# A new order for the opening of a decoder layer on one core: keys, values, queries, with identity products first

## The chip, the cores and the metric

The kernel runs on one core of a Trainium2 chip. The metric is device microseconds of one execution; the median of several runs is compared. TensorE (PE), VectorE (DVE), ScalarE (ACT), GpSimd (POOL) and the DMA queues of SyncE (SP) and ScalarE work in parallel and wait for each other through semaphores.

## The reference

Input x is 16 sequences of 128 tokens of 128 numbers. Four stages follow each other, each with a residual and a layer norm: a gated convolution mixer, a decoder block of self-attention and cross-attention (16 heads of 64) with a feed-forward of 512, and a last feed-forward with one expert for each of the first 16 tokens. The change concerns the mixer, at the start of the kernel:

```python
x = jnp.einsum('bld,de->ble', u, W_in) + b_in
x = jnp.swapaxes(x, 1, 2)
uc = dw_causal_conv(x, short_w, short_b)
q, k, v = (uc[:, :D], uc[:, D:2 * D], uc[:, 2 * D:])
v = k * v
v = dw_causal_conv(v, inner_w, inner_b)
y = q * v
y = jnp.swapaxes(y, 1, 2)
return jnp.einsum('bld,de->ble', y, W_out) + b_out
```

## The kernel before, in words

One block holds five instruction streams, written out by hand, one for each engine; each runs strictly in its written order, so the order of the lines is the schedule. Sequences go through the mixer in 8 pairs m (two sequences, 256 columns) and through the attentions as items n = 0 to 31 (16 of self-attention, then 16 of cross-attention).

Input projection and three-tap convolution of the mixer are one operation: VectorE multiplies W_in by each tap (`first_weights`, L1162), and nine matmuls per part c (three taps; each product in three, of high and low halves of fp32) add up in one PSUM bank (`projection`, L608 to L610). Part 0 are the queries, 1 the keys, 2 the values. Operands are split into a rounded high half, by ScalarE (`w_hi` L969, `x_high` L872, `weight_high` L903), and a low rest, by VectorE (`first_weights_low` L1168, `x_low` L1155, `weight_low` L1239).

A pair then goes like this: ScalarE copies each part out of its bank into C with the bias (`projected`, L881); GpSimd corrects the first two columns of all three parts (L1565) and multiplies keys by values into KV (`keys_values`, L1569); VectorE runs the four-tap inner convolution into G (`inner_convolution`, L1194, L1198); GpSimd multiplies the queries into yT (`gate`, L1576); TensorE makes the output product (`mixer_output`, L622), into the bank of the keys; VectorE adds the residual (`mixer_residual`, R, L1207), to which GpSimd has added the output bias (`output_bias`, L1583), and takes the moments (L1214 to L1221); GpSimd raises to the power -1/2 (`mixer_deviation`, L1591); VectorE makes the shift (`mixer_shift`, L1227), ScalarE the normalised rows N (L891); TensorE transposes them (L634), ScalarE and VectorE take the high and low halves x1 (L899, `x1_low` L1234). The units of the first items follow (`unit`, L72 to L74: two head pairs of queries or keys for two items), copied out by ScalarE (queries, L827) and VectorE (keys, `k_out`, L1099); with the key units of the first two turns comes `scores(0)` (L551), then `maxima` on VectorE (L1081), which adds the mask `maskb` (made at L1402), and so on through a loop over the items, in which pairs 3 to 7 of the mixer are woven in.

The three parts of a pair use two banks: queries bank 4, keys bank 5, values bank 4 again. So the values of a pair wait for the copy of its queries, and a pair waits for the copies of the one before:

```python
C_BANK, OUT1_BANK, X1T_BANK = (4, 5, 4), 5, W_BANK
wait(pe, c_ok, (3 * m, 3 * m, 3 * m + 1)[c])
```

The opening of TensorE is: projections of pair 0, then of pair 1, output product of pair 0, projections of pair 2, transposes of pair 0, output product of pair 1, eight units, scores of item 0. Small bias terms (`tap_biases`, `first_biases`, L1173 to L1184) are VectorE's, between the weights.

## Time and profile before

| | us |
|---|---|
| median of 3 runs (501.26 to 502.74) | 501.43 |
| the profiled execution, its time | 501.12 |
| its span in the trace | 499.2 |
| TensorE busy in the span | 470.6 (94%) |
| VectorE busy | 385.0 (77%) |
| ScalarE busy | 366.8 (73%) |
| GpSimd busy | 251.9 (50%) |

The time of the execution has about 1.9 us around the span of the trace. All later times count from the start of the span. TensorE's digits in the slices of the page stand at 4, 7 and 8 for the first three slices (37 us) and at 9 from the fourth to the last but two; DMA is at 8, 7 and 4 tenths in the first three slices and near nothing after them, with two exceptions.

### The profile page before, as it was taken

The page shows a single profiled execution, that of the slowest core. Times are in us where ns is not written, and L with a number is a line of the kernel's source. Part 1 is how long each engine was busy: PE and PEld are TensorE (multiplying, and loading weights), DVE is VectorE, ACT ScalarE, POOL GpSimd, SP SyncE. Part 2 cuts the span into 40 slices and gives each one's busy share as a digit, 9 for nine tenths or more (in the row PEclk, how much of TensorE's full clock was granted, in tenths as well). Part 3 has the DMA queues.
Part 4 walks back from the last instruction along what each step waited for, and adds up shares of the span by engine and source line. Part 5 has one row for each costly group of instructions (what it writes and reads, how often), then busy time and mean ns, then how long its engine had stood idle before and what let it go on. Part 6 is the DMA issues. An engine that isn't in the chain of part 4 may idle for free.

```text
span 499.2 us, 14097 instructions
## 1 busy us (share of the span) xinstructions
PE 470.6 (94%) x4644; PEld 431.5 (86%) x4644; DVE 385.0 (77%) x1852; ACT 366.8 (73%) x1390; POOL 251.9 (50%) x342
## 2 busy tenths in 40 slices
PE   4788999999999999999999999999999999999894
PEld 4678889999999999999999999999999997798672
DVE  4768778898888877887787777777777777538866
ACT  3547887868677788877778887777777777836763
POOL 1545357675565654555545454444554455633432
PEclk9999999999999999999999999999999999999987
DMA  8740000000000004000000000000000000400003
GB/s 242 233 195 2 1 3 1 2 2 2 1 3 1 2 2 126 1 4 1 3 1 2 2 2 1 3 1 3 3 1 3 1 2 3 169 1 0 7 13 90
DMA packets 15720, 14.18 MB, mean 28 GB/s; under 512 B 2848, under 2 KB 13344, under 8 KB 15520
## 3 DMA queue, kind: packets, MB, share of 16 engines
q1 hardware_dynamic: 14080, 12.81, 8.2%
q8 instruction: 38, 0.62, 0.5%
q10 hardware_dynamic: 1568, 0.47, 0.5%
q14 instruction: 34, 0.28, 0.2%
HBM read 12.10 MB, written 1.18 MB: 27 GB/s over the span
## 4 chain that ended last, share of the span: by engine, by line
PE 73%; DVE 13%; ACT 5%; issue 3%; DMA 2%; POOL 2%; SPq 1%; POOLq 0%; DVEq 0%; ACTq 0%
PE late_bank L582 10%; PE late_bank L534 10%; PE late_bank L551 10%; PE late_bank L566 10%; PE late_bank L72 8%; PE late_bank L74 8%; PE late_bank L73 8%; ACT P L817 3%; DVE P L1081 3%; DMA x<-in_xT 2%; PE late_bank L591 1%; DVE G L1198 1%; DVE ffstats L1253 1%; PE late_bank L608 1%; PE late_bank L610 1%
## 5 line engine op out<-in xcount | busy, mean ns | idle before, releaser
L817 ACT ACTIVATE P<-P,at_negmax 128x128 f32<-128x128 f32 x512 | 198.9, 396 | 79.1 <-DVE at_negmax L1081 79.1
L1530 POOL TENSOR_TENSOR P<-P,at_inv 128x512 f32<-128x512 f32 x128 | 136.6, 1078 | 123.2 <-DVE at_inv L1091 123.1
L1107 DVE COPY at_PT<-late_bank 128x512 f32<-128x512 f32 x128 | 87.7, 688 | 35.1 <-PE late_bank L534 34.9
L1081 DVE CUSTOM_DVE_ANT_0 P<-late_bank,maskb 128x128 f32<-128x128 f32 x512 | 110.5, 286 | 2.7 <-PE late_bank L551 2.7
L817 ACT ACTIVATION_READ_ACCUMULATOR P<-P,at_negmax 128x1 f32 x512 | 100.1, 195 | 0.0
L534 PE MATMUL late_bank<-ident,P 128*128 128x128 f32 x512 | 76.4, 273 | 2.0 <-DVE at_negmax L1081 1.0
L534 PEld LDWEIGHTS late_bank<-ident,P 128*128 128x128 f32 x512 | 59.8, 140 | 8.5 <-issue 4.0
L551 PE MATMUL late_bank<-at_k,at_q 64*128 64x128 f32 x1024 | 65.8, 278 | 0.9 <-DVE at_k L1099 0.9
L551 PEld LDWEIGHTS late_bank<-at_k,at_q 64*128 64x128 f32 x1024 | 59.7, 188 | 4.8 <-issue 1.2
L566 PE MATMUL late_bank<-at_PT,V 128*64 128x128 f32 x1024 | 63.0, 276 | 0.0
L566 PEld LDWEIGHTS late_bank<-at_PT,V 128*64 128x64 f32 x1024 | 55.2, 137 | 3.9
L1099 DVE COPY at_k<-late_bank 128x512 f32<-128x512 f32 x64 | 44.2, 691 | 8.1 <-PE late_bank L74 7.0
L1081 DVE DVE_READ_ACCUMULATOR2_ANT at_negmax<- 128x1 f32 x512 | 42.7, 83 | 0.0
L827 ACT ACTIVATE at_q<-late_bank 128x512 f32<-128x512 f32 x64 | 37.7, 589 | 4.0 <-PE late_bank L74 4.0
L1548 POOL TENSOR_TENSOR at_N<-at_N,row_ln_g 128x128 f32<-128x128 f32 x32 | 14.7, 460 | 49.8 <-DVE at_N L1132 49.8
L836 ACT ACTIVATE V<-late_bank 128x512 f32<-128x512 f32 x64 | 37.6, 587 | 0.0
L844 ACT ACTIVATE at_OT<-late_bank 128x512 f32<-128x512 f32 x64 | 34.3, 587 | 2.9 <-PE late_bank L566 2.9
L608 PE MATMUL late_bank<-xT_hi,w_hi 128*128 128x256 f32 x72 | 22.8, 317 | 11.2 <-DVE xT_lo L1155 7.1
L582 PE MATMUL late_bank<-wo_sa,at_OT 128*128 128x128 f32 x256 | 31.3, 276 | 0.6 <-DVE x1T_lo L1234 0.6
L582 PE MATMUL late_bank<-wo_ca,at_OT 128*128 128x128 f32 x256 | 31.2, 275 | 0.0
L582 PEld LDWEIGHTS late_bank<-wo_sa,at_OT 128*128 128x128 f32 x256 | 29.9, 192 | 1.0 <-issue 1.0
L582 PEld LDWEIGHTS late_bank<-wo_ca,at_OT 128*128 128x128 f32 x256 | 29.9, 192 | 0.1
(195 smaller groups left out, 1055.4 us busy)
## 6 DMA issues: line engine op xcount, KB each, us to landing
ctxT_raw<-in_ctxT SPq DMA_DIRECT2D x1, 1024.0 KB, 8.8
out<-xres SPq DMA_DIRECT2D x4, 224.0 KB, 2.6
x<-in_xT SPq DMA_DIRECT2D x1, 768.0 KB, 9.5
xres<-in_x SPq DMA_DIRECT2D x1, 768.0 KB, 14.0
tap_rows<-in_short_wT SPq DMA_DIRECT2D x3, 192.0 KB, 4.9
sa_wq_raw<-in_sa_wq SPq DMA_DIRECT2D x1, 512.0 KB, 7.4
sa_wk_raw<-in_sa_wk SPq DMA_DIRECT2D x1, 512.0 KB, 8.5
sa_wv_raw<-in_sa_wv SPq DMA_DIRECT2D x1, 512.0 KB, 9.8
```

The source lines that it names most:

```text
L72: nc.tensor.matmul(out, w.hi[wsel], x.hi[xsel], start=first, stop=False)
L73: nc.tensor.matmul(out, w.hi[wsel], x.lo[xsel], start=False, stop=False)
L74: return nc.tensor.matmul(out, w.lo[wsel], x.hi[xsel], start=False, stop=True)
L534: last = nc.tensor.transpose(banks[T_BANK[g % 2]][:, h * 128:(h + 1) * 128], P[:, n % 2, HQ * g + h, :], k.ident[:])
L551: last = nc.tensor.matmul(score_bank(h), q[rows, t % 2, h // 2, pair], kk[rows, t % 2, h // 2, pair], start=True, stop=True)
L566: last = nc.tensor.matmul(banks[O_BANK[h // 8]][part:part + 64, h // 2 % 4 * 128:(h // 2 % 4 + 1) * 128], V[:, n % 2, h * DH:(h + 1) * DH] ...
L582: last = nc.tensor.matmul(banks[W_BANK][:, 0:128], OT[:, n % 2, c, :], out_w[att(n)][:, c, :], start=(c == 0), stop=(c == H // 2 - 1))
L817: last = nc.scalar.activation(P[:, n % 2, h, :], P[:, n % 2, h, :], ACT.Exp, scale=-1.0, bias=negmax[:, n % 2, h:h + 1], accum_out=total[: ...
L1081: last = nc.vector.tensor_tensor_reduce(P[:, n % 2, h, :], score_bank(h), k.maskb[:, cols(n)], scale=1.0, scalar=3.0e38, op0=ALU.add, op1= ...
L1099: nc.vector.tensor_copy(kk[:, t % 2, u - 1:u + 1, :], banks[UNIT_BANK[1]][:].rearrange("p (h l) -> p h l", h=2)).then_inc(k_ok, 1)
L1107: nc.vector.tensor_copy(PT[:, HQ * g:HQ * g + HQ, :], banks[T_BANK[g % 2]][:].rearrange("p (h l) -> p h l", h=HQ)).then_inc(pt_ok, 1)
L1530: nc.gpsimd.tensor_tensor(tile, tile, inv[:, n % 2, HQ * g:HQ * g + HQ].unsqueeze(2).to_broadcast([128, HQ, 128]), ALU.mult).then_inc(norm ...
```

## The change

The parts of the first three pairs go in the order keys, values, queries (`FIRST_ORDER`), in all engines, with weights, taps and loads in that order too. For these pairs each part has a bank of its own (keys 5, values 4, queries bank 6, the bank of the attention's values), and a part waits for the copy of the same part of the pair before. Twelve products of the identity with itself stand ahead of the first projection, into bank 3. The edge correction is done in two instructions, keys and values ahead of their product, queries ahead of the gate, in all eight pairs. The small bias operations go to GpSimd. The output product of pair 0 stands between values and queries of pair 1, that of pair 1 after the first query unit. The other engines' lists are reordered accordingly; the mask operation moves from before the first convolution to between two key copies.

```diff
-        C_BANK, OUT1_BANK, X1T_BANK = (4, 5, 4), 5, W_BANK
+        C_BANK, FIRST_C_BANK, OUT1_BANK, X1T_BANK = (4, 5, 4), (V_BANK, 5, 4), 5, W_BANK
+        FIRST_PAIRS, FIRST_ORDER = 3, (1, 2, 0)
+        def place(m, c):
+
+            return 3 * m + (FIRST_ORDER.index(c) if m < FIRST_PAIRS else c)
...
-            for n in SA[:2]:
-                sp.dma_start(k.raw[n][:], io[n]).then_inc(ld_w[n], 16)
             tokens = io["x"].rearrange("b p d -> p b d")
+            sp.dma_start(k.raw[SA[0]][:], io[SA[0]]).then_inc(ld_w[SA[0]], 16)
             sp.dma_start(k.xres[:, 0:GRP], tokens[:, 0:GRP]).then_inc(ld_xres[0], 16)
+            sp.dma_start(k.raw[SA[1]][:], io[SA[1]]).then_inc(ld_w[SA[1]], 16)
...
-                wait(pe, c_ok, (3 * m, 3 * m, 3 * m + 1)[c])
+                if m < FIRST_PAIRS:
+                    wait(pe, c_ok, place(m - 1, c) + 1)
+                else:
+                    wait(pe, c_ok, (3 * m, 3 * m, 3 * m + 1)[c])
...
             pe.wait_ge(ident_ok, 1)
+            for _ in range(12):
+                nc.tensor.matmul(banks[3][:, 0:128], k.ident[:], k.ident[:], start=True, stop=True)
             pe.wait_ge(pads_ok, 2)
-            for m in (0, 1):
-                for c in range(3):
-                    projection(-1, m, c)
+            for c in FIRST_ORDER:
+                projection(-1, 0, c)
+            projection(-1, 1, 1)
+            projection(-1, 1, 2)
             mixer_output(-1, 0)
-            for c in range(3):
-                projection(-1, 2, c)
+            projection(-1, 1, 0)
+            projection(-1, 2, 1)
             x1_transposes(-1, 0)
+            projection(-1, 2, 2)
+            unit(-2, 0)
             mixer_output(-1, 1)
-            for j in range(4):
+            projection(-1, 2, 0)
+            for j in range(1, 4):
                 unit(-2, j)
...
+            nc.scalar.dma_start(w_out[:], io["W_out"]).then_inc(ld_tok, 16)
+            row_broadcast(nc, act, b_out[:], io["b_out"]).then_inc(ld_tok, 16)
             row_broadcast(nc, act, k.mask_raw[:], io["mask"].rearrange("b p -> (b p)")).then_inc(ld_mask, 16)
-            row_broadcast(nc, act, b_out[:], io["b_out"]).then_inc(ld_tok, 16)
-            nc.scalar.dma_start(w_out[:], io["W_out"]).then_inc(ld_tok, 16)
...
             x_high(1)
-            for c in range(3):
+            for c in FIRST_ORDER:
                 projected(0, c)
+            weight_high(SA[0])
+            projected(1, 1)
+            projected(1, 2)
             x_high(2)
-            weight_high(SA[0])
-            for c in range(3):
-                projected(1, c)
+            projected(1, 0)
             weight_high(SA[1])
-            projected(2, 0)
+            mixer_normal(0)
             projected(2, 1)
-            mixer_normal(0)
+            x1_high(0)
             projected(2, 2)
-            x1_high(0)
-            x_high(3)
             weight_high(SA[2])
             q_out(-2, 0)
+            projected(2, 0)
+            x_high(3)
...
+            def edges(m, parts):
+                count = parts.stop - parts.start
+                part = C[:, m % 2, parts, :, 0:2]
+                nc.gpsimd.tensor_tensor(part, part, edge[:, parts].unsqueeze(2).to_broadcast([128, count, PAIR, 2]),
+                                        ALU.add).then_inc(fix_ok, 1)
...
-                pool.wait_ge(c_ok, 3 * (m + 1))
-                part = C[:, m % 2, :, :, 0:2]
-                nc.gpsimd.tensor_tensor(part, part, edge[:].unsqueeze(2).to_broadcast([128, 3, PAIR, 2]),
-                                        ALU.add).then_inc(fix_ok, 1)
-                pool.wait_ge(fix_ok, m + 1)
+                pool.wait_ge(c_ok, 3 * m + (2 if m < FIRST_PAIRS else 3))
+                edges(m, np.s_[1:3])
+                pool.wait_ge(fix_ok, 2 * m + 1)
...
+                pool.wait_ge(c_ok, 3 * (m + 1))
+                edges(m, np.s_[0:1])
+                pool.wait_ge(fix_ok, 2 * (m + 1))
                 pool.wait_ge(g_ok, m + 1)
...
-            pool.wait_ge(edge_ok, 2)
+            pool.wait_ge(zeros_ok, 1)
+            tap_biases()
             keys_values(0)
+            gate(0)
             output_bias(0)
-            gate(0)
```

VectorE, from the second x split of the opening to the residual of pair 0 and on to the low half of x1 (the rows of the moments are left out; `xT_lo` is a split of x, `sa_wq_lo` of the query weights, `sa_wk_lo` of the key weights; what stands in brackets is what the instruction waits for). Before:

```order
L1155 TENSOR_TENSOR xT_lo<-x1,xT_hi 128x2x128 [waits mx_xhi]
L1402 TENSOR_SCALAR maskb<-mask_raw 128x2048 [waits mx_ld_mask]
L1194 TENSOR_SCALAR G<-KV,inner,inner_b 128x256 [waits mx_ld_inner,mx_kv_ok]
L1198 SCALAR_TENSOR_TENSOR G<-KV,inner,G 128x256 [waits mx_g_part] x3
L1155 TENSOR_TENSOR xT_lo<-x1,xT_hi 128x2x128 [waits mx_xhi]
L1239 TENSOR_TENSOR sa_wq_lo<-sa_wq_raw,sa_wq_hi 128x1024 [waits mx_w_hi]
L1207 TENSOR_TENSOR R1<-late_bank5,xres 128x256 [waits mx_xb_ok,mx_o1_mm]
L1194 TENSOR_SCALAR G<-KV,inner,inner_b 128x256 [waits mx_y_ok,mx_kv_ok]
L1198 SCALAR_TENSOR_TENSOR G<-KV,inner,G 128x256 [waits mx_g_part] x3
L1227 SCALAR_TENSOR_TENSOR shift1<-mv1,rstd1 128x2 [waits mx_rstd1_ok]
L1239 TENSOR_TENSOR sa_wk_lo<-sa_wk_raw,sa_wk_hi 128x1024 [waits mx_w_hi]
L1234 TENSOR_TENSOR x1T_lo<-late_bank7,x1T_hi 128x256 [waits mx_x1hi]
```

and now:

```order
L1191 TENSOR_TENSOR w3_lo<-w3_raw,w3_hi 128x3x128 [waits mx_whi]
L1201 TENSOR_SCALAR G<-KV,inner,inner_b 128x256 [waits mx_ld_inner,mx_kv_ok]
L1205 SCALAR_TENSOR_TENSOR G<-KV,inner,G 128x256 [waits mx_g_part] x3
L1246 TENSOR_TENSOR sa_wq_lo<-sa_wq_raw,sa_wq_hi 128x1024 [waits mx_w_hi]
L1214 TENSOR_TENSOR R1<-late_bank5,xres 128x256 [waits mx_xb_ok,mx_o1_mm]
L1178 TENSOR_TENSOR xT_lo<-x1,xT_hi 128x2x128 [waits mx_xhi]
L1234 SCALAR_TENSOR_TENSOR shift1<-mv1,rstd1 128x2 [waits mx_rstd1_ok]
L1201 TENSOR_SCALAR G<-KV,inner,inner_b 128x256 [waits mx_y_ok,mx_kv_ok]
L1205 SCALAR_TENSOR_TENSOR G<-KV,inner,G 128x256 [waits mx_g_part] x3
L1241 TENSOR_TENSOR x1T_lo<-late_bank7,x1T_hi 128x256 [waits mx_x1hi]
L1246 TENSOR_TENSOR sa_wk_lo<-sa_wk_raw,sa_wk_hi 128x1024 [waits mx_w_hi]
```

The mask operation is gone from here, the shift stands ahead of the second convolution instead of behind it, and the low half of x1 behind that convolution, ahead of the key weights.

VectorE again, from the residual of pair 1 to the first scores (the moments left out again; `at_k` are the key copies, `sa_wv_lo` the value weights). Before:

```order
L1207 TENSOR_TENSOR R1<-late_bank5,xres 128x256 [waits mx_n1_ok,mx_xb_ok,mx_o1_mm]
L1099 COPY at_k<-late_bank1 128x512 [waits at_u_mm] x2
L1239 TENSOR_TENSOR sa_wv_lo<-sa_wv_raw,sa_wv_hi 128x1024 [waits mx_w_hi]
L1099 COPY at_k<-late_bank1 128x512 [waits at_u_mm]
L1227 SCALAR_TENSOR_TENSOR shift1<-mv1,rstd1 128x2 [waits mx_rstd1_ok]
L1099 COPY at_k<-late_bank1 128x512 [waits at_u_mm]
```

and now:

```order
L1214 TENSOR_TENSOR R1<-late_bank5,xres 128x256 [waits mx_n1_ok,mx_xb_ok,mx_o1_mm]
L1122 COPY at_k<-late_bank1 128x512 [waits at_u_mm]
L1246 TENSOR_TENSOR sa_wv_lo<-sa_wv_raw,sa_wv_hi 128x1024 [waits mx_w_hi]
L1122 COPY at_k<-late_bank1 128x512 [waits at_u_mm]
L1421 TENSOR_SCALAR maskb<-mask_raw 128x2048 [waits mx_ld_mask]
L1234 SCALAR_TENSOR_TENSOR shift1<-mv1,rstd1 128x2 [waits mx_rstd1_ok]
L1122 COPY at_k<-late_bank1 128x512 [waits at_u_mm]
L1178 TENSOR_TENSOR xT_lo<-x1,xT_hi 128x2x128 [waits mx_xhi]
L1122 COPY at_k<-late_bank1 128x512 [waits at_u_mm]
```

The value weights are one key copy earlier, and the mask operation and a split of x stand between the key copies.

TensorE around the output product of pair 0 (`late_bank5<-w_out,yT`). Before:

```order
L608 MATMUL late_bank4<-xT_hi,w3_hi 128x256
L609 MATMUL late_bank4<-xT_lo,w3_hi 128x256
L610 MATMUL late_bank4<-xT_hi,w3_lo 128x256
L622 MATMUL late_bank5<-w_out,yT 128x128 [waits mx_c_ok,mx_y_ok,mx_ld_tok]
L622 MATMUL late_bank5<-w_out,yT 128x128
L608 MATMUL late_bank4<-xT_hi,w3_hi 128x256 [waits mx_c_ok,mx_xlo]
```

and now:

```order
L621 MATMUL late_bank4<-xT_hi,w3_hi 128x256
L622 MATMUL late_bank4<-xT_lo,w3_hi 128x256
L623 MATMUL late_bank4<-xT_hi,w3_lo 128x256
L638 MATMUL late_bank5<-w_out,yT 128x128 [waits mx_c_ok,mx_y_ok,mx_ld_tok]
L638 MATMUL late_bank5<-w_out,yT 128x128
L621 MATMUL late_bank6<-xT_hi,w3_hi 128x256 [waits mx_c_ok]
```

Before, the product comes after the nine matmuls of pair 1's values and ahead of pair 2's queries, in bank 4. Now it comes ahead of pair 1's queries, in bank 6.

## Rows read from the trace of the kernel before

**Rows 1.** Windows: stretch, us, busy of PE, PEld, DVE, ACT, POOL, clock, DMA

```profile
7.00:12.00 5.00, 4.93 (x24) 4.96 (x25) 4.18 (x11) 2.19 (x5) 0.00 (x0) 1.00 1.01 358
34.00:60.00 26.00, 23.54 (x210) 21.61 (x211) 19.76 (x96) 20.04 (x81) 10.79 (x14) 1.00 0.00 1
60.00:450.00 390.00, 386.73 (x4039) 359.82 (x4038) 307.26 (x1521) 301.85 (x1217) 210.84 (x285) 1.00 0.04 11
```

**Rows 2.** Timeline of PE: start us, duration us, line, operation [idle before]

```profile
7.07 0.55 PE L608 MATMUL late_bank<-xT_hi,w_hi 128*128 128x256 f32 x1 [7.07 <-DVE xT_lo L1155]
...
11.47 0.39 PE L610 MATMUL late_bank<-xT_hi,w_lo 128*128 128x256 f32 x1
11.69 0.29 PE L608 MATMUL late_bank<-xT_hi,w_hi 128*128 128x256 f32 x1
11.81 0.28 PE L609 MATMUL late_bank<-xT_lo,w_hi 128*128 128x256 f32 x1
...
18.49 0.61 PE L622 MATMUL late_bank<-w_out,yT 128*128 128x128 f32 x4
...
24.86 0.39 PE L72 MATMUL late_bank<-x1T_hi,sa_wq_hi 128*128 128x256 f32 x1
...
34.09 2.06 PE L551 MATMUL late_bank<-at_k,at_q 64*128 64x128 f32 x32 [0.88 <-DVE at_k L1099]
```

**Rows 3.** The timeline of ACT in the opening

```profile
12.61 0.47 ACT L881 ACTIVATE C<-late_bank,conv_bias 128x256 f32<-128x256 f32 x1 [0.85 <-PE late_bank L610]
15.53 0.42 ACT L872 ACTIVATE xT_hi<-x 128x256 fp32r<-128x256 f32 x1 [2.44 <-DMA x<-in_xT]
```

**Rows 4.** The timeline of POOL in the opening

```profile
13.26 0.21 POOL L1565 TENSOR_TENSOR C<-C,edge 128x12 f32<-128x12 f32 x1 [10.61 <-ACT C L881]
13.55 0.74 POOL L1569 TENSOR_TENSOR KV<-C 128x256 f32<-128x256 f32 x1
...
16.77 0.84 POOL L1576 TENSOR_TENSOR yT<-C,G 128x256 f32<-128x256 f32 x1 [1.79 <-DVE G L1198]
...
20.65 0.81 POOL L1591 TENSOR_TENSOR rstd<-mv,half_neg 128x2 f32<-128x2 f32 x1 [0.38 <-DVE mv L1221]
22.53 1.71 POOL L1576 TENSOR_TENSOR yT<-C,G 128x256 f32<-128x256 f32 x1 [1.07 <-DVE G L1198]
```

**Rows 5.** The timeline of DVE in the opening

```profile
10.70 1.22 DVE L1402 TENSOR_SCALAR maskb<-mask_raw 128x2048 bf16<-128x2048 uint8 x1
...
16.94 1.75 DVE L1239 TENSOR_TENSOR sa_wq_lo<-sa_wq_raw,sa_wq_hi 128x1024 fp32r<-128x1024 f32 x1
19.13 0.42 DVE L1207 TENSOR_TENSOR R<-late_bank,xres 128x256 f32<-128x256 f32 x1 [0.44 <-PE late_bank L622]
...
20.48 0.41 DVE L1194 TENSOR_SCALAR G<-KV,inner,inner_b 128x256 f32<-128x256 f32 x1
20.93 1.52 DVE L1198 SCALAR_TENSOR_TENSOR G<-KV,inner,G 128x256 f32<-128x256 f32 x3
...
22.37 0.15 DVE L1227 SCALAR_TENSOR_TENSOR shift<-mv,rstd 128x2 f32<-128x2 f32 x1
22.44 1.22 DVE L1239 TENSOR_TENSOR sa_wk_lo<-sa_wk_raw,sa_wk_hi 128x1024 fp32r<-128x1024 f32 x1
...
26.19 0.43 DVE L1207 TENSOR_TENSOR R<-late_bank,xres 128x256 f32<-128x256 f32 x1 [0.68 <-issue]
...
27.53 0.69 DVE L1099 COPY at_k<-late_bank 128x512 f32<-128x512 f32 x1
29.28 0.69 DVE L1099 COPY at_k<-late_bank 128x512 f32<-128x512 f32 x1 [1.07 <-PE late_bank L74]
29.89 1.70 DVE L1239 TENSOR_TENSOR sa_wv_lo<-sa_wv_raw,sa_wv_hi 128x1024 fp32r<-128x1024 f32 x1
```

**Rows 6.** The line L446, the load of x for pair 1

```profile
L446 SPq DMA_DIRECT2D x<-in_xT x1: 486/486/486, 3.2 to 3.2; - x1
DMA to landing us min/median/max: 6.3/6.3/6.3
```

94 lines of the change are left out of this document (49 added, 45 removed).

## The prediction

> **What bounds the kernel now.** I read the windows by stage first, for the stage in which TensorE is not full. From 60 to 450 us it is busy for 386.7 of 390 us, so nothing can be won there by order; between 34 and 60 us 2.5 us are missing, and the opening before that is thin [rows 1]. Then the timeline of each engine from the start to the first scores. TensorE begins at 7.07 us, gives the first output product at 18.49, the first query unit at 24.86 and the first scores at 34.09 [rows 2]. What follows the scores hangs on them through relative waits only, all loads that it needs being long on their way, so I count what the change does to the 34.09 and carry it to the end.
>
> Along that path the reader is to see three things. The queries, keys and values of pair 0 are all needed before GpSimd may multiply keys by values: the third copy starts at 12.61, the product KV ends at 14.29 [rows 3, 4]. ScalarE then waits for the large x load until 15.53 [rows 3], with the copies of pair 1 queued behind it, and TensorE holds the first output product behind pair 1, though its operand yT is done at 17.61 [rows 2, 4]. Last, VectorE: its shift for the first layer norm is issued at 22.37, behind a whole convolution of pair 1 (20.48 to 22.45) [rows 5]. From 27.53 VectorE and TensorE hand each other key units, with waits such as the 1.07 us at 29.28 [rows 5].
>
> **The change, step by step.** Times are of the profiled execution.
>
> *Identity products.* They wait for the identity alone, and no row shows when they start. TensorE does nothing before 7.07 in any case. Two output products of the same shape and type leave four matmul records, spaced about like those of 256 columns (0.61 us for four, of which 0.28 is the last one's own) [rows 2]. So twelve make 24 records, at the early spacing of 0.22 (11.47 to 11.69) 5.3 us at most. So they should be over about when the first projection is ready, at the same 7.07 as before. Matmuls of 256 columns start 0.22 us apart up to 11.69, and 0.12 from there [rows 2]: the engine worked at half its rate (the 1.2 GHz level) for 4.6 us from its first matmul, then at the full one. If the products do that stretch, every projection costs 9 x 0.12 = 1.1 us instead of 9 x 0.21 = 1.9. Bounds: worth the whole of it, or nothing. I take the whole, since they are as long and as dense as the stretch that did it before.
>
> *Keys and values first.* The weights of the second part are combined, split and subtracted as before, without the small bias operations among them, but with the third part's combination (0.56) ahead of the second subtraction. I put the values' weights at 8.9, their product at 8.9 + 1.1 + 0.2 of drain = 10.2 and their copy (0.47) at 10.7. GpSimd needs only these two: 0.3 for the edge and 0.7 for KV [rows 4] give 11.9 against 14.29. The convolution takes 1.97 (20.48 to 22.45) [rows 5], to 13.9. The five small bias operations on GpSimd cost about 0.3 each by the spacing of its smallest one (13.26 to 13.55) [rows 4], 1.5 in all, before anyone needs them: nothing.
>
> *The port.* VectorE goes on at 13.9 with the low part of the query weights, GpSimd with yT. Where VectorE began first, its 1.22 (22.44) made yT take 1.71 (22.53); where GpSimd began first, yT took 0.84 and the weights 1.75 (16.77, 16.94) [rows 4, 5]. In the new order they stand next to each other and VectorE need not wait for a signal: I take 1.6 for yT, to 15.5; the other bound, 0.84, is a rival.
>
> *Output product between projections.* It comes at 15.6 instead of 18.49, so R at 16.3 instead of 19.13, 2.8 earlier; the bias addition that it also needs, as large as KV's product (0.7), follows yT and ends at 16.2. GpSimd's power ended at 21.46 (20.65 and 0.81), 2.33 behind the start of R, and the shift could have followed there [rows 4, 5]; it is now ahead of the convolution and comes 2.4 behind R, at 18.7. From shift to first query unit took 2.49 (22.37 to 24.86). Now the convolution of pair 1 stands between shift and the low part of x1, 18.7 + 1.97 + 0.42: again 21.2. The first unit is **3.7 us earlier**.
>
> *What is given back.* The residual of pair 1 waits for GpSimd's addition of the output bias, which stands behind keys times values of pair 2; and that product's projection now comes after the transposes, at 19.9, so its copy ends at 21.7. The key weights' 1.22 us on VectorE (from 21.1) then hold GpSimd's port; edge, KV and bias addition end at 24.1, R of pair 1 starts at 24.2 instead of 26.19: 2.0 earlier. The first key copy starts at 25.6 instead of 27.53.
>
> From there before: 6.56 us to the scores. Now: key copy 0.6, low value weights 1.2 (as at 22.44), key copy 0.6, then the **mask multiplication, 1.22, which before ran at 10.70 while VectorE had to wait for KV anyway** [rows 5] and here stands on the path, then as before from the end of the value weights (31.59) to the scores, 2.5. The moved x split (0.42) fits into the wait for the last key unit. Sum 6.1; if the mask operation begins beside a GpSimd addition, 0.45 more, as the 1.70 at 29.89 and the 1.75 at 16.94 against 1.22 show for the weights. So the scores start between 31.7 and 32.2. I take 32.2, since both long operations that stood beside GpSimd's were held: **1.9 us earlier**.
>
> By the Trainium skill (page "SBUF — State Buffer", section "SBUF: two separate sides") VectorE and GpSimd share a port pair as an exclusive lock, which a VectorE operation takes if it has two SBUF inputs or runs in a two-port mode; the mask operation has one input. By that rule it would be held only if its mode is such a one, and no row here shows it beside GpSimd. If it is not, the saving is 2.4.
>
> *Nothing for the rest.* The edge correction is now two GpSimd instructions per pair, 8 more in all at about 0.3. GpSimd is busy for 210.8 of 390 us [rows 1], and the added one runs before the convolution's result is there. Of the loads, first x of GRP sequences and key weights change places and the mask goes last of three: each is needed later than it lands. Should GpSimd be late all eight times, 2.4 us would be gone.
>
> Sum: 501.12 - 1.9 = 499.2 for the profiled execution. The median of the three runs stands 0.3 above it, at 501.43, so I forecast **499.5**. A measurement of this kernel tells about 0.3% (1.5 us) from no change; faster means below 499.9.
>
> **Rivals.**
>
> A. *The identity products do not raise the rate* before the projections. For: no row shows such products. Against: the rate changed once in the opening and stayed through the gaps after it. Then values follow keys at 9.1 to 11.1, KV is 1.1 later, and 0.8 are left: 500.6. Chance 0.14.
>
> B. *GpSimd gets the port.* If query weights reach ScalarE late, yT begins first and ends 0.9 earlier; with the mask operation not held, another 0.45. Up to 3.2 saved, 2.8 likely: 498.6. Chance 0.14.
>
> C. *The saving is taken up later.* The 2.5 us of missing TensorE time from 34 to 60 us [rows 1] may hide waits that do not move, or the added edge instructions fall on the path. 0.2 to 0.9 left: 500.8. Chance 0.12.
>
> D. *Slower: the second x pair.* On both ScalarE and VectorE the split of x of pair 1 now stands ahead of the copies and the query weights of pair 0. That load was issued at 3.2 and took 6.3, to 9.5 [rows 6], with the DMA engines full (share 1.01 from 7 to 12 us) [rows 1]. It decides from about 9.8, one for one: a landing at 11.7 leaves nothing, at 13.3 the kernel is 1.6 slower, 503.0. For: the rearranged queue of ScalarE loads beside it. Against: the mask's 256 KB, which ran beside it before, now follow 128 KB of others. Chance 0.05, with 0.02 more for anything else that is late.
>
> **How the numbers follow.** The main case has 0.53, with its own range of 499.0 to 500.0 from the bounds of the port and 0.3 us of seams in so long a chain. 498.4 to 501.2 takes in A, B and C with the spread of the runs; D is outside. Faster: 0.48 of the main case and B, 0.62. Same: the rest of the main case, A and C, 0.31. Slower: 0.07.
>
> **What would show it.** In the profile after: matmul spacing of 0.12 from the first projection (A if 0.21); first output product near 15.6, yT of 1.6 (B if 0.8); first query unit near 21.2; R of pair 1 near 24.2; the mask operation at 28 with 1.2 or 1.7; scores near 32.2, and every later landmark shifted by the same amount (C if less at 60 us than at 34). I am wrong if the output product is earlier but the scores are not, or if the first projection starts after 7.1 because the identity products still run.

## The result, and the profile after

| | before | after |
|---|---|---|
| median of 7 runs each, us | 501.43 (500.66 to 502.74) | 499.21 (497.63 to 501.00) |
| the profiled execution, its time and span | 501.12 / 499.2 | 499.44 / 497.6 |
| first scores of item 0 | 34.09 | 32.57 |

The ratio of the runs, after to before, is 0.9949, with a 95% interval of 0.9928 to 0.997: faster by 2.2 us, or between 0.3% and 0.7%. The forecast was 499.5.

The timeline of PE in the profile after, against [rows 2] (start us, duration us, line, operation, idle before):

```profile
1.56 5.49 PE L735 MATMUL late_bank<-ident 128*128 128x128 f32 x24 [1.56 <-POOL ident L1658]
7.23 0.55 PE L621 MATMUL late_bank<-xT_hi,w_hi 128*128 128x256 f32 x1 [0.18 <-DVE xT_lo L1178]
7.58 0.38 PE L622 MATMUL late_bank<-xT_lo,w_hi 128*128 128x256 f32 x1
7.80 0.28 PE L623 MATMUL late_bank<-xT_hi,w_lo 128*128 128x256 f32 x1
7.92 0.28 PE L621 MATMUL late_bank<-xT_hi,w_hi 128*128 128x256 f32 x1
...
15.78 0.68 PE L638 MATMUL late_bank<-w_out,yT 128*128 128x128 f32 x4 [1.72 <-issue]
...
21.36 0.39 PE L72 MATMUL late_bank<-x1T_hi,sa_wq_hi 128*128 128x256 f32 x1
...
32.57 0.68 PE L561 MATMUL late_bank<-at_k,at_q 64*128 64x128 f32 x7 [0.88 <-DVE at_k L1122]
```

The identity products fill 1.56 to 7.05. The first projection starts at 7.23; its first two matmuls still take 0.35 and 0.22 us to the next, and from 7.80 on they follow at 0.12 us. The output product comes 2.71 earlier, the first unit 3.50, the scores 1.52: more than half of the lead is given back between unit and scores.

The timeline of POOL, against [rows 4]:

```profile
10.94 0.20 POOL L1581 TENSOR_TENSOR C<-C,edge 128x8 f32<-128x8 f32 x1 [3.80 <-ACT C L903]
11.23 0.73 POOL L1592 TENSOR_TENSOR KV<-C 128x256 f32<-128x256 f32 x1
...
14.11 1.57 POOL L1602 TENSOR_TENSOR yT<-C,G 128x256 f32<-128x256 f32 x1 [1.12 <-DVE G L1205]
...
22.10 0.83 POOL L1581 TENSOR_TENSOR C<-C,edge 128x8 f32<-128x8 f32 x1 [0.32 <-ACT C L903]
23.02 0.74 POOL L1592 TENSOR_TENSOR KV<-C 128x256 f32<-128x256 f32 x1
23.71 0.73 POOL L1609 TENSOR_TENSOR xres<-xres,b_out 128x256 f32<-128x256 f32 x1
...
28.25 1.80 POOL L1627 TENSOR_TENSOR x<-N,row_ln_b 128x256 f32<-128x256 f32 x1
```

and of DVE, against [rows 5]:

```profile
5.01 0.56 DVE L1185 TENSOR_TENSOR w_raw<-w_in,tap_rows 128x384 f32<-128x384 f32 x1 [5.01 <-DMA tap_rows<-in_short_wT]
...
13.88 1.22 DVE L1246 TENSOR_TENSOR sa_wq_lo<-sa_wq_raw,sa_wq_hi 128x1024 fp32r<-128x1024 f32 x1
16.50 0.42 DVE L1214 TENSOR_TENSOR R<-late_bank,xres 128x256 f32<-128x256 f32 x1 [1.40 <-PE late_bank L638]
...
21.23 1.65 DVE L1246 TENSOR_TENSOR sa_wk_lo<-sa_wk_raw,sa_wk_hi 128x1024 fp32r<-128x1024 f32 x1
24.54 0.42 DVE L1214 TENSOR_TENSOR R<-late_bank,xres 128x256 f32<-128x256 f32 x1 [1.67 <-issue]
...
25.88 0.68 DVE L1122 COPY at_k<-late_bank 128x512 f32<-128x512 f32 x1
26.48 1.21 DVE L1246 TENSOR_TENSOR sa_wv_lo<-sa_wv_raw,sa_wv_hi 128x1024 fp32r<-128x1024 f32 x1
...
28.23 1.22 DVE L1421 TENSOR_SCALAR maskb<-mask_raw 128x2048 bf16<-128x2048 uint8 x1
29.37 0.70 DVE L1234 SCALAR_TENSOR_TENSOR shift<-mv,rstd 128x2 f32<-128x2 f32 x1
29.99 0.68 DVE L1122 COPY at_k<-late_bank 128x512 f32<-128x512 f32 x1
...
31.73 0.69 DVE L1122 COPY at_k<-late_bank 128x512 f32<-128x512 f32 x1 [0.72 <-PE late_bank L74]
```

KV ends at 11.96 instead of 14.29. Wherever a long weight split of VectorE meets GpSimd, one of the two is long: the query weights (13.88) begin first and yT takes 1.57; the key weights (21.23) take 1.65 beside the end of the second pair's yT, and the edge correction at 22.10 has 0.83 for eight columns' work. The mask operation at 28.23 took its plain 1.22, but GpSimd's addition beside it took 1.80, and the shift behind it, of 128 x 2 numbers, 0.70. The first row is the start of the whole chain: the moment at which the first taps land.

The windows from 34 us on (us, then busy of PE, PEld, DVE, ACT, POOL, clock, DMA), against [rows 1]:

```profile
34.00:60.00 26.00, 23.59 (x216) 21.65 (x214) 21.00 (x103) 21.52 (x84) 10.39 (x13) 1.00 0.01 2
60.00:450.00 390.00, 386.72 (x4019) 359.24 (x4017) 308.12 (x1525) 301.74 (x1215) 211.72 (x289) 1.00 0.04 11
```

Nothing changed there. The scores of items 0, 1 and 5 start at 32.57, 46.94 and 101.40 where they started at 34.09, 48.43 and 102.90: the lead stays at 1.5 us.

### The profile page after: what moved, and what is told of

The parts are those of the page before. It is cut to its first block, busy times and chain, and to the rows that moved or that the text cites. A ratio compares the mean times of both kernels' runs of the same rounds, so it can differ in the third digit from the quotient of the medians.

```text
span 497.6 us, 14153 instructions
## 1 busy us (share of the span) xinstructions
PE 471.0 (95%) x4668; PEld 433.1 (87%) x4668; DVE 384.3 (77%) x1847; ACT 366.9 (74%) x1390; POOL 257.2 (52%) x355
## 4 chain that ended last, share of the span: by engine, by line
PE 70%; DVE 15%; ACT 5%; issue 4%; DMA 2%; POOL 2%; SPq 1%; POOLq 0%; DVEq 0%; ACTq 0%
PE late_bank L592 11%; PE late_bank L544 10%; PE late_bank L561 10%; PE late_bank L576 10%; PE late_bank L72 8%; PE late_bank L74 8%; PE late_bank L73 8%; ACT P L839 3%; DVE P L1104 3%; DVE ffstats L1260 2%; PE late_bank L601 1%; DMA x<-in_xT 1%; PE late_bank L621 1%; PE late_bank L622 1%; PE late_bank L623 1%
## 5 line engine op out<-in xcount | busy, mean ns | idle before, releaser
L1114 DVE RECIPROCAL at_inv<-at_total 128x4 f32<-128x4 f32 x128 | 21.0, 170 | 9.4 <-ACT P L839 9.4
```

## The experiments

Single times lie up to 1 to 3 us from their median (once 4 us), as much as most of the effects, so the traces carry the verdicts, one traced execution for each kernel. A single trace has a scatter too: the first taps landed at 4.88 us in the trace before, at 5.01 in that after, and between 5.11 and 5.72 in the experiments. This table counts from that landing, VectorE's first product; when the first experiments were planned, landmarks were counted from the start of the span, and all expectations but that of e11 are in those times.

| | taps land | output product | first unit | R of pair 1 | first key copy | scores | median us (runs) | ratio to before, interval |
|---|---|---|---|---|---|---|---|---|
| before | 4.88 | 13.61 | 19.98 | 21.31 | 22.65 | 29.21 | 501.43 (7) | 1 |
| after | 5.01 | 10.77 | 16.35 | 19.53 | 20.87 | 27.56 | 499.21 (7) | 0.9949 (0.9928 to 0.997) |
| e1_no_identity | 5.32 | 11.81 | 18.77 | 21.37 | 22.71 | 29.42 | 501.56 (10) | 1.0005 (0.9986 to 1.0025) |
| e2_kv_waits_all | 5.44 | 11.65 | 20.19 | 25.77 | 27.11 | 34.07 | 506.56 (4) | 1.0101 (1.0057 to 1.0145) |
| e3_product_behind | 5.11 | 10.51 | 16.94 | 19.50 | 20.84 | 27.54 | 499.58 (10) | 0.9969 (0.9941 to 0.9998) |
| e4_two_banks | 5.44 | 10.64 | 16.22 | 19.39 | 20.73 | 27.42 | 499.52 (10) | 0.9959 (0.9935 to 0.9983) |
| e12_biases_back | 5.63 | 10.64 | 16.22 | 19.40 | 20.74 | 27.43 | 500.82 (10) | 0.9982 (0.9959 to 1.0005) |
| e5_mask_late | 5.56 | 10.52 | 16.64 | 19.38 | 20.72 | 26.82 | 498.87 (9) | 0.9941 (0.9915 to 0.9967) |
| e6_bias_early | 5.54 | 10.63 | 16.74 | 18.21 | 19.99 | 27.06 | 500.15 (10) | 0.9956 (0.9932 to 0.998) |
| e7_both | 5.17 | 10.94 | 17.63 | 19.09 | 20.87 | 27.37 | 499.87 (12) | 0.995 (0.9927 to 0.9973) |
| e8_weights_behind | 5.72 | 9.65 | 15.67 | 18.83 | 20.17 | 26.87 | 499.64 (10) | 0.9962 (0.9942 to 0.9982) |
| e9_keep_busy | 5.30 | 10.49 | 16.07 | 19.25 | 20.59 | 27.28 | 499.72 (12) | 0.9948 (0.9921 to 0.9976) |
| e10_three_moves | 5.63 | 10.51 | 16.09 | 18.28 | 19.62 | 25.73 | 498.34 (12) | 0.9937 (0.9915 to 0.9958) |
| e11_four_moves | 5.34 | 9.67 | 15.69 | 17.87 | 19.21 | 25.33 | 497.62 (8) | 0.9923 (0.9891 to 0.9954) |

The ratios are each against runs of the kernel before made beside them, whose medians were 501.38 to 501.98. e9's twelve runs include one of 943.20 us, which the ratio leaves out (its median without it is 499.36); the runs of the kernel before include one of 1619.77 and one of 1182.75 us, left out in the same way.

How far can a difference in this table be trusted? From the output product to the scores the change, e4, e9 and e12 take 16.79, 16.78, 16.79 and 16.79 us. From the taps to the output product, though, the change, e5, e6, e9 and e10, which hardly differ up to there, have 10.77, 10.52, 10.63, 10.49 and 10.51: the change's own is the latest. So a gain against it, counted from the taps, can be up to 0.28 too large. Counted from the output product, the scores come 0.49 earlier in e5, 0.36 in e6 and 1.57 in e10.

### Parts of the change undone, one at a time

**e1_no_identity**: the twelve identity products are taken away.

```diff
             pe.wait_ge(ident_ok, 1)
-            for _ in range(12):
-                nc.tensor.matmul(banks[3][:, 0:128], k.ident[:], k.ident[:], start=True, stop=True)
             pe.wait_ge(pads_ok, 2)
```

> The changed kernel without the twelve identity products; all else is kept. My theory (each landmark hands its lead on to the next): the first nine matmuls of the keys and those of the values run 0.21 us apart, the copy of the values of pair 0 comes about 1.0 later (11.4 instead of 10.39), and first output product (16.8), residual of pair 1 (25.6) and scores of item 0 (33.6 instead of 32.57) are all 1.0 to 1.1 later; the time is 1.1 above the changed kernel's, some 1.1 below the kernel before. Rival 1 (the products are worth nothing, the order alone does it): scores at 32.6, same time as the changed kernel. Rival 2 (the higher rate alone does it): the whole saving is gone, scores at 34.1, time as before.

The whole gain went: 501.56, and scores 0.2 later from the taps than before the change. By its time this is what rival 2 said; my theory had half of that loss. Its PE timeline has the slow start again, behind the first projection instead of ahead of it:

```profile
7.51 0.55 PE L621 MATMUL late_bank<-xT_hi,w_hi 128*128 128x256 f32 x1 [7.51 <-DVE xT_lo L1176]
7.86 0.42 PE L622 MATMUL late_bank<-xT_lo,w_hi 128*128 128x256 f32 x1
8.07 0.42 PE L623 MATMUL late_bank<-xT_hi,w_lo 128*128 128x256 f32 x1
```

They stay 0.21 apart until 11.7, and the output product is 1.04 later than after the change. That was expected (against the 10.49 of e9 it is 1.3 later). The rest was not: from output product to first unit it lost another 1.38 (6.96 against 5.58). Its windows (us, PE busy, clock, DMA) show why:

```profile
16.00:18.00 2.00, 0.87 (x7) 1.00 0.57 110
18.00:20.00 2.00, 1.38 (x9) 0.65 0.68 130
20.00:22.00 2.00, 2.00 (x11) 0.50 0.84 232
22.00:24.00 2.00, 2.00 (x11) 0.50 0.91 232
24.00:26.00 2.00, 2.00 (x14) 0.64 0.95 314
```

The granted clock fell to 0.50, the 1.2 GHz level, after a thin stretch. That is a second effect, to which the section on the hardware comes back. The products alone are thus worth 1.0 to 1.3 us in the landmarks, and what else this execution lost is not theirs for certain. The median of ten runs is 2.35 above the change's; how much of that is such stretches in the executions that were not traced stays open.

**e2_kv_waits_all**: GpSimd waits for all three copies again ahead of keys times values.

```diff
-                pool.wait_ge(c_ok, 3 * m + (2 if m < FIRST_PAIRS else 3))
+                pool.wait_ge(c_ok, 3 * m + 3)
```

> The changed kernel, but GpSimd's product of keys and values waits for all three copies of its pair, as before the change. My theory: KV of pair 0 starts 1.6 later (12.8 instead of 11.23), the first output product at 17.3 instead of 15.78, and since the queries of pair 2 are now made last, KV of pair 2 and behind it the bias addition of pair 1 come 4 later, so the scores start near 36.8, 2.7 later than in the kernel before: time 2 to 3 above the kernel before. Rival (keys and values first is not what brings it): scores within 0.3 of 32.57, time as the changed kernel.

The output product moved by 0.9, less than the 1.5 expected, but R of pair 1 by 6.2. The time is 5.1 above the kernel before, about twice what I had expected. POOL's timeline shows where:

```profile
20.71 0.21 POOL L1581 TENSOR_TENSOR C<-C,edge 128x8 f32<-128x8 f32 x1 [3.04 <-ACT C L903]
...
29.43 0.20 POOL L1581 TENSOR_TENSOR C<-C,edge 128x8 f32<-128x8 f32 x1 [4.07 <-ACT C L903]
29.71 0.73 POOL L1592 TENSOR_TENSOR KV<-C 128x256 f32<-128x256 f32 x1
30.40 0.72 POOL L1609 TENSOR_TENSOR xres<-xres,b_out 128x256 f32<-128x256 f32 x1
```

For pair 2 the third copy is that of the queries, whose projection the change has put behind the first unit and the second output product. GpSimd waited 4.07 us for it, and the bias addition for pair 1 is queued behind; for the queries of pair 1 it had already waited 3.04. A part of the loss comes from the clock, which stood near 0.50 in three stretches of this opening (around 18, 25 and 36 us); this trace can't separate it. The four runs took 504.09 to 508.41, all slower than the change's slowest. So the new order on TensorE and the shorter wait on GpSimd only work together: with the old wait it is slower than before by 1.0%.

**e3_product_behind**: the output product of pair 0 goes back behind pair 1.

```diff
-            mixer_output(-1, 0)
             projection(-1, 1, 0)
+            mixer_output(-1, 0)
             projection(-1, 2, 1)
```

> The changed kernel with the output product of pair 0 behind the queries' projection of pair 1 again. My theory: the projection then fills TensorE's idle time from 14.0 to 15.8, the output product still starts at 15.8 because yT ends there, and nothing moves: scores at 32.5 to 32.6, time as the changed kernel. Rival (the product's place between the projections is worth what TensorE has queued ahead of it): the output product 1.1 later, scores 1.1 later, time 1.1 above the changed kernel.

Output product, R of pair 1 and scores are where they were, within the scatter said above (27.54 against 27.56): its place is worth nothing that can be seen, since its operand yT is ready only at 15.68 in the profile after, and the nine matmuls that it would wait behind fit into TensorE's idle time ahead of that. The first unit was 0.6 later, in a stretch at a clock of 0.50 from 18 to 20 us; R of pair 1, which waits for GpSimd, hardly felt it (8.99 behind the output product instead of 8.76).

**e4_two_banks**: values and queries of the first pairs share bank 4 again.

```diff
-        C_BANK, FIRST_C_BANK, OUT1_BANK, X1T_BANK = (4, 5, 4), (V_BANK, 5, 4), 5, W_BANK
+        C_BANK, FIRST_C_BANK, OUT1_BANK, X1T_BANK = (4, 5, 4), (4, 5, 4), 5, W_BANK
...
-                    wait(pe, c_ok, place(m - 1, c) + 1)
+                    wait(pe, c_ok, (3 * m + 2, place(m - 1, 1) + 1, 3 * m)[c])
```

> The changed kernel with two banks instead of three for the first pairs: values and queries share bank 4, with the waits that this needs. My theory: the queries of pair 0 start at 10.9 instead of 10.56 and the values of pair 1 behind the copy of the queries, both with slack of more than 0.5 before GpSimd wants them: scores at 32.4 to 32.9, time as the changed kernel. Rival (the third bank is what lets the projections run on): output product or residual of pair 1 later by 1 or more, and the scores with them, at 33.6 or more.

27.42 against 27.56: the third bank is worth nothing that can be seen here. Once the queries stand last, sharing costs them a wait that nobody behind them feels.

**e12_biases_back**: the five small bias operations back on VectorE.

```diff
             first_weights(2)
+            tap_biases()
             first_weights(0)
             first_weights_low(2)
+            first_biases()
             x_low(1)
```

> The changed kernel with the five small bias operations back on VectorE, between the products of taps, as they stood before. They took 0.07 to 0.2 us of VectorE each, and VectorE has idle stretches of 0.20 (at 7.7 us) and 0.66 (at 9.0) there. Theory (moving them was worth little in itself): the tap products of the values move by 0.1 to 0.3, first output product at 15.9 to 16.1, scores at 32.7 to 32.9, median 499.3 to 499.6. Rival (VectorE is what the first projections wait for, so that all of their 0.8 counts): scores at 33.2 to 33.5, median 500.0.

Landmarks of 10.64, 16.22 and 27.43 are those of e4 to 0.01. Counted from the taps, this part is worth nothing. The times stand higher than that, and above both expectations: a median of 500.82, 1.6 above the change's, with an interval of the ratio (0.9959 to 1.0005) that overlaps the change's. The scores of the profiled execution (33.06 from the start of the span) account for 0.5 of it, by taps that landed 0.62 later; the rest stays open. It isn't the clock alone: its five runs with a mean clock of 0.994 or more took 498.78 to 500.31, the change's three 497.63 to 499.44.

### What gives the lead back: moves beyond the change

**e5_mask_late**: the mask operation right ahead of the first maxima.

```diff
             k_out(-2, 3)
-            vec.wait_ge(ld_mask, 16)
-            nc.vector.tensor_scalar(k.maskb[:], k.mask_raw[:], MASKED, None, ALU.mult).then_inc(mask_ok, 1)
             mixer_shift(1)
             k_out(-1, 1)
             x_low(3)
             k_out(-1, 3)
+            vec.wait_ge(ld_mask, 16)
+            nc.vector.tensor_scalar(k.maskb[:], k.mask_raw[:], MASKED, None, ALU.mult).then_inc(mask_ok, 1)
             maxima(0, 0)
```

> The changed kernel with the mask multiplication moved behind the last key copy of the opening, right ahead of the first maxima, where VectorE waits 1.5 us for the scores. My theory (in the changed kernel it stands on the path for 1.22, and through GpSimd's hold of the port for 0.5 more, of which unit waits cover a part): third key copy at 29.1 instead of 29.99, scores at 31.4 to 31.7 instead of 32.57, first maxima 0.9 to 1.1 earlier; time 1.0 below the changed kernel. Rival (it fills a wait in the changed kernel too): scores within 0.2 of 32.57.

From first key copy to scores it took 6.10 instead of 6.69. DVE's timeline, and the row of POOL that the mask operation had stood beside:

```profile
28.64 0.15 DVE L1234 SCALAR_TENSOR_TENSOR shift<-mv,rstd 128x2 f32<-128x2 f32 x1
29.79 0.69 DVE L1122 COPY at_k<-late_bank 128x512 f32<-128x512 f32 x1 [1.00 <-PE late_bank L74]
```

```profile
28.65 0.74 POOL L1627 TENSOR_TENSOR x<-N,row_ln_b 128x256 f32<-128x256 f32 x1
```

Without the mask operation beside it GpSimd's addition takes 0.74 instead of 1.80, and the shift is back at 0.15. So 1.22 + 0.55 us left the path; 1.00 of it came back as a wait for TensorE's unit, which before the change stood there as 1.07 [rows 5]. What stays is 0.6 behind the first key copy. The median is only 0.3 below the change's, where I had expected 1.0; its three runs at a mean clock of 0.994 took 497.34 to 497.48, the change's at 0.994 or more 497.63 to 499.44. The mask operation now runs at 32.15, beside the scores, and nobody waits for it. Between the output product and the first unit this execution lost 0.5 to a clock of 0.50 from 18 to 20 us, but R of pair 1, which waits for GpSimd, lost only 0.1 by it.

**e6_bias_early**: GpSimd adds the output bias for pair 1 ahead of its gate.

```diff
             mixer_deviation(0)
+            output_bias(1)
             gate(1)
             keys_values(2)
-            output_bias(1)
```

> The changed kernel with GpSimd's output bias addition of pair 1 ahead of the gate of pair 1, in its idle time from 19 to 21 us, instead of behind keys times values of pair 2. My theory (that addition is what the residual of pair 1 waits for): residual of pair 1 at 23.0 to 23.3 instead of 24.54, first key copy at 24.7 to 24.9 instead of 25.88, scores at 31.6 to 31.8: time 0.9 below the changed kernel. Rival (TensorE's own work up to the key unit is the bound there): scores within 0.2 of 32.57.

Counted from the taps, R of pair 1 comes 1.3 earlier, as expected, the key copy 0.9, the scores 0.5 (0.36 if counted from the output product); from the start of the span the scores stand at 32.60, which reads like the rival. The median of 500.15 is 0.9 above the change's instead of below it, with intervals that overlap, so no gain is shown in the time. DVE again:

```profile
19.25 0.69 DVE L1234 SCALAR_TENSOR_TENSOR shift<-mv,rstd 128x2 f32<-128x2 f32 x1 [0.60 <-POOL rstd L1617]
...
25.53 0.69 DVE L1122 COPY at_k<-late_bank 128x512 f32<-128x512 f32 x1 [0.35 <-PE late_bank L74]
26.14 1.61 DVE L1246 TENSOR_TENSOR sa_wv_lo<-sa_wv_raw,sa_wv_hi 128x1024 fp32r<-128x1024 f32 x1
```

The bias addition started at 19.20, 0.05 ahead of the shift, which took 0.69 for 0.15: the whole second convolution is 0.5 later. Further on the key copy waits for its unit, and the value weights (1.61) now meet a GpSimd operation.

**e7_both**: e5 and e6 together.

```diff
             mixer_deviation(0)
+            output_bias(1)
             gate(1)
             keys_values(2)
-            output_bias(1)
...
             k_out(-1, 3)
+            vec.wait_ge(ld_mask, 16)
+            nc.vector.tensor_scalar(k.maskb[:], k.mask_raw[:], MASKED, None, ALU.mult).then_inc(mask_ok, 1)
             maxima(0, 0)
```

> Both moves together: mask multiplication ahead of the first maxima, bias addition of pair 1 ahead of the gate. My theory: they shorten different stretches of one chain but meet the waits between key copies and key units, so less than the sum: scores at 30.8 to 31.1 instead of 32.57; time 1.6 below the changed kernel, near 497.6, 3.8 below the kernel before. Rival (a later wait takes it up): scores near 31, but item 2's scores less than 1 earlier than 58.29.

The scores stand at 27.37 from the taps, a smaller gain than either move gave alone, and the median is 499.87: neither the theory nor the rival foresaw that. Here the output product itself ran at half the clock: the window from 16 to 18 us has 0.55, four records took 1.12 us, and R of pair 0 followed 1.16 behind it instead of 0.72.

```profile
16.00:18.00 2.00, 1.89 (x9) 0.55 0.63 144
18.00:20.00 2.00, 2.00 (x11) 0.60 0.51 115
20.00:22.00 2.00, 1.21 (x11) 1.00 0.93 270
```

The first shift has 0.70 again, and the first key copy its wait of 0.35. So this trace can't tell what the two moves give together with the clock at 1.00; the two runs with a mean clock of 0.994 took 496.88 and 497.02, near the 497.6 of the theory. Two places are left at which the lead is lost, and e10 was made from them.

**e8_weights_behind**: the low part of the query weights behind the first residual's moments.

```diff
-            weight_low(SA[0])
             mixer_residual(0)
             mixer_statistics(0)
             x_low(2)
+            weight_low(SA[0])
```

> The changed kernel with the low part of the query weights behind the moments and the x split of pair 0 on VectorE instead of ahead of the residual. My theory of the port: GpSimd's yT of pair 0 takes 0.75 to 0.85 instead of 1.57 and the first output product starts at 14.9 instead of 15.78; but the 1.2 us of the weights then meet GpSimd's power or the shift, so the first query unit stays within 0.4 of 21.36 and the scores within 0.3 of 32.57: time as the changed kernel. Rival 1 (yT is slow for another reason than VectorE's operation beside it): yT 1.6 still. Rival 2 (the lead of the output product carries through): scores 0.9 earlier.

In POOL's timeline the first gate is no longer held:

```profile
14.54 0.72 POOL L1602 TENSOR_TENSOR yT<-C,G 128x256 f32<-128x256 f32 x1 [1.86 <-DVE G L1205]
```

0.72 instead of 1.57 brings the output product 1.1 forward, the first unit 0.68, the scores 0.69; against e9's execution, whose landmarks are the earliest of the undisturbed ones, it is 0.84, 0.40 and 0.41. From the start of the span they stood at 32.59, like the change's, and I first read that as a lead that doesn't carry; but in this execution the taps landed 0.7 later. Counted from them, about half of it carries, which is between my theory and rival 2; the other half is lost at the shift, which is issued at 18.90, behind the query weights. What was left was lost again in the time of this execution (500.75): the clock fell to 0.50 at 33 to 36 us, and item 1's scores, 14.4 behind item 0's elsewhere, came 15.65 behind. The median of ten runs, 499.64, is not below the change's.

**e9_keep_busy**: 18 more identity products in TensorE's gaps.

```diff
             projection(-1, 1, 2)
+            keep_busy(6)
             mixer_output(-1, 0)
             projection(-1, 1, 0)
+            keep_busy(3)
             projection(-1, 2, 1)
...
+            keep_busy(5)
             unit(-2, 3)
...
+            keep_busy(2)
             unit(-1, 3)
+            keep_busy(2)
             scores(0)
```

> The changed kernel with 18 more 128x128 identity products into the unused bank: 6 in TensorE's idle stretch ahead of the first output product (13.9 to 15.8 us), 3 ahead of the third pair's keys (17.4 to 18.3), 5, 2 and 2 in the gaps between the units and ahead of the first scores. At the full clock one takes 0.22 us, so that each group fits into its gap (1.3 of 1.9, 0.66 of 0.9, 1.1 of 1.3, 0.44 of 0.67 and of 0.88). Theory (the stretches at 1.2 GHz in the opening, which five of the profiled executions had, follow idle gaps of TensorE): the opening runs at a granted clock of 1.00 throughout, the landmarks stand where the changed kernel's stand (scores of item 0 at 32.4 to 32.8), and the median is 498.5 to 499.3. Rival (the low clock does not come from these gaps): a stretch at 0.5 appears in the opening as in the others, and there each product takes twice as long and delays what is behind it, scores at 33 to 34, median 499.5 to 500.5.

Inconclusive. The profiled execution had a clock of 1.00 throughout the opening, and the fillers delayed no landmark (27.28). But the median is in the rival's range, and the runs say that low mean clocks did not go away: five had a mean clock of 0.994 to 0.997 and 497.68 to 498.05 us, the six others 0.985 to 0.99 and 499.36 to 501.67. Only one execution is traced, so where those six lost it isn't known. Several kernels without fillers had a clean opening as well.

**e10_three_moves**: mask late; bias addition behind the gate, so that it doesn't meet the shift; the first key unit ahead of pair 2's queries, so that the key copy doesn't wait.

```diff
             gate(1)
-            keys_values(2)
             output_bias(1)
+            keys_values(2)
...
             mixer_output(-1, 1)
+            unit(-2, 1)
             projection(-1, 2, 0)
-            for j in range(1, 4):
+            for j in range(2, 4):
```

> The changed kernel with three steps moved: the mask's conversion right before maxima(0, 0), the bias addition for pair 1 on GpSimd between gate(1) and keys_values(2), and the second unit of product on TensorE (keys, unit(-2, 1)) ahead of projection(2, 0). Theory (the chain to the first scores goes through the residual of pair 1 and the four copies of keys, and each of the three takes something out of it): residual of pair 1 at 22.9 to 23.7 (was 24.54), first copy of keys at 24.3 to 25.0 (was 25.88), first scores 5.3 to 6.1 behind it plus 0.1, at 30.0 to 31.2 (was 32.57), median 497.2 to 498.4. Rival (as in the two moves run together before: what is taken out at one place comes back at the next, by the shared port or by a unit that is waited for): scores at 32.0 to 32.6 and 499 to 500. A stretch of half clock in the opening would add 0.5 to 1.3 to these landmarks.

The theory holds, if the landmarks are counted from the taps: R of pair 1 is 1.25 earlier, the key copy 1.25, the scores 1.83 (1.57 from the output product). From the start of the span all three lie 0.16 to 0.25 above its ranges, with taps that landed 0.62 later. The median of 498.34 lies in the range too. At R a wait is left:

```profile
21.41 0.73 POOL L1603 TENSOR_TENSOR yT<-C,G 128x256 f32<-128x256 f32 x1 [2.05 <-issue]
22.10 1.72 POOL L1610 TENSOR_TENSOR xres<-xres,b_out 128x256 f32<-128x256 f32 x1
```

The bias addition is held by the key weights, and R waits for it. The third key copy still waits 1.00 for its unit.

**e11_four_moves**: e10 with the edit of e8.

```diff
-            weight_low(SA[0])
             mixer_residual(0)
             mixer_statistics(0)
             x_low(2)
+            weight_low(SA[0])
```

> The three moves (mask late, bias addition of pair 1 behind gate(1), keys' unit ahead of projection(2, 0)) and a fourth: the first part of the queries' weights on VectorE behind mixer_statistics(0) and x_low(2), so that it no longer holds GpSimd's product for the first gate. Landmarks are counted from the landing of the first taps (VectorE's first product), since that differs by 0.7 us among the executions: the changed kernel has 10.77 to the first output product, 16.35 to the first unit and 27.56 to the first scores; the three moves 10.51, 16.09 and 25.73; the fourth move alone 9.65, 15.67 and 26.87. Theory (what the fourth move gives is carried through to the scores, 0.4 to 0.7 us, since the next steps follow one another without slack): 9.5 to 9.8, 15.3 to 15.7, and scores at 25.0 to 25.4; median 497.3 to 498.2. Rival (it is given back at the next wait): 9.5 to 9.8 for the output product, but scores at 25.6 to 25.8, and 498.2 to 498.8.

9.67, 15.69 and 25.33: the fourth move's lead of 0.84 at the output product is 0.40 at the scores, at the lower end of the theory. Half of it is lost at the shift, which now stands behind the query weights. DVE's timeline to the last key copy:

```profile
17.41 1.22 DVE L1247 TENSOR_TENSOR sa_wq_lo<-sa_wq_raw,sa_wq_hi 128x1024 fp32r<-128x1024 f32 x1
18.54 0.15 DVE L1235 SCALAR_TENSOR_TENSOR shift<-mv,rstd 128x2 f32<-128x2 f32 x1
...
23.21 0.42 DVE L1215 TENSOR_TENSOR R<-late_bank,xres 128x256 f32<-128x256 f32 x1 [0.69 <-PE late_bank L638]
...
29.83 0.69 DVE L1123 COPY at_k<-late_bank 128x512 f32<-128x512 f32 x1 [0.74 <-PE late_bank L74]
```

With 497.62 and 0.9923 (0.9891 to 0.9954) it has the lowest median of all kernels here, and it beats the one before. Against the changed kernel the intervals overlap; what speaks for it is the trace, 2.2 us at the scores, and the runs at a mean clock of 0.994 to 0.996: 497.58, 496.09, 496.38 and 496.06 against the change's 499.44, 498.90 and 497.63.

## Why the prediction was right

*The main case happened, with its mechanism.* First output product forecast at 15.6, measured 15.78; first unit 21.2, measured 21.36; R of pair 1 24.2, measured 24.54; scores 32.2, measured 32.57. The profiled time was to be 499.2 and was 499.44, and the median 499.5 and was 499.21. That the median came this close is in part luck, with runs that lie 3 us apart. So is it that both traces that are compared, before and after, have a granted clock of 1.00 in the opening: six of the other twelve fell to 0.50 there. Of the 0.37 that the scores were late, 0.13 is the landing of the taps (5.01 against 4.88), which no term could hold.

*Identity products.* They ran from 1.56 and were over 0.18 ahead of the first projection, as forecast. Two of its matmuls were still slow, so "0.12 from the first projection" was not quite so. That they do the slow stretch is shown by e1. The step's statement that they last as long as the stretch that did it before (4.6 us) was too sure: here the rate rose 6.1 us after the first of them, and in e11 3.5 us after. Their end was close: the forecast gave them 5.3, they took 5.49.

*Keys and values first.* KV forecast to end at 11.9, measured 11.96. The terms written down add up to 11.7; the rest is the time from the copy's end to the edge correction, which the sum took along without a word. e2 shows that this is the part without which all else is a loss. I had priced it at pair 0 alone, where undoing it costs 0.9; pair 2, where it costs the most, stood in no term.

*The port.* yT was forecast at 1.6 and took 1.57; rival B asked what 0.84 would bring, and e8 and e11 answer: 0.4 to 0.7 at the scores in e8, 0.40 in e11, less than the 0.9 that B counted, since half of it is lost again at the shift. The mask operation was **the step that failed in form and not in size**: I let it take 0.45 more beside a GpSimd addition. It took 1.22, and the operation that paid was the shift behind it, with 0.55 more. The Trainium skill (page "SBUF — State Buffer", section "SBUF: two separate sides") has the port pair as an exclusive lock. The trace agrees: GpSimd's addition began 0.02 behind the mask operation and took 1.80 instead of 0.72, and the shift then waited for it; in e5 and e10, with the mask operation elsewhere, the same addition took 0.74 and 0.73. So the mask operation does take the lock, with its one input; what my text left open is thereby closed, and the saving of 2.4 for the other case could not come.

*Output product between projections.* 2.8 earlier was right (2.71), the reason in the heading was not: e3 shows that the place is worth nothing that can be seen, and the earliness is that of yT. Third bank and small biases, which I costed at nothing as gains too, are at nothing by the landmarks of e4 and e12; e12's higher times stay open.

*What is given back.* The lead was 1.65 at R of pair 1 (forecast 2.0) against 3.50 at the first unit, by the bias addition that queues behind key weights, edge and KV. The key weights took 1.65 and not the forecast 1.22, since they met the end of yT. From key copy to scores it took 6.69, where the forecast had 6.6 and the kernel before 6.56. e5, e6 and e10 take some of this back: 0.7, 0.5 and 1.8 us from the taps, 0.5, 0.4 and 1.6 from the output product.

*The rivals.* A fell with the first row, and its price for the early rate was about right (1.04 to 1.3 in e1 against 1.1). C did not happen: the lead is 1.49 to 1.52 at every item looked at. D did not: the load of pair 1 took 5.9 and landed at 9.1.

## What to carry to other kernels

In a chain through several engines, look for what each long operation stands beside: a VectorE operation that takes the shared port costs whoever comes next, even a shift of 128 x 2 numbers, so the cost shows on a row other than the one that was moved. A lead at one landmark is kept only as far as no queue behind it holds the next operand, so move the queue's items with it; one edit at a time gave 0.4 to 0.7, three that fit together 1.6 to 1.8. And before two traces are compared, count from the event that starts the chain, here a load that lands at 4.9 to 5.7 us.

## What the runs showed of the hardware that I had not expected

**The granted clock falls inside a thin opening.** In six of the fourteen profiled executions it fell to 0.50, the 1.2 GHz level, in the first 40 us: e1, e2 (three times), e3, e5, e7 and e8. TensorE had been busy but with gaps before it: 0.87 of 2 us in e1's window ahead of the fall. A stretch cost 0.5 (e5) to 1.4 us (e1) at the landmark behind it. The executions of the kernel before, of the changed kernel, e4, e6 and e9 to e12 kept 1.00. The longest idle stretch of TensorE between 12 and 20 us was 1.85 (e3) to 3.28 us (e2) in the five in which the clock fell before 20 us, and 0.67 (e9) to 2.05 us (e10) in those that kept 1.00. The two ranges overlap, so the gaps alone don't decide it.

**The mean clock goes with most of the scatter.** Among the executions of e9, of e10 and of e11 those at a mean clock of 0.994 or more took 497.7 to 498.1, 497.4 to 498.1 and 496.1 to 497.6 us; those at 0.982 to 0.987 took 500.7 to 501.7, 499.2 to 500.9 and 498.9 to 499.2. That is 1.3 to 4 us for one kernel, as much as the change brought. Where in these executions the clock was low isn't known, since one of each is traced.

**The early half rate is not in the granted clock.** In the first 3.5 to 6 us of TensorE's work the matmuls are twice as far apart (0.21 and 0.12 us), while the clock column reads 1.00 there, before [rows 1] and after. It ended 4.6 us after the first matmul before the change, 4.2 after it in e1, and some 6.1 after the first identity product in the changed kernel (between 7.58 and 7.80); the twelve products took the full 5.49 us in six of the twelve executions that have them and 4.49 (e11) to 5.27 in the others. So only in half of them did the slow stretch end among the products, in e11 some 3.5 us after the first.
